# Turning the combine weights and the probabilities by VectorE's 32x32 blocks and transfers instead of TensorE

## The reference, cut to what matters

```python
xn = layernorm(x)
# attention: width 128, window of 32 tokens to either side
h = relu(xn @ nm_w1 + nm_b1);  m = h @ nm_w2 + nm_b2
q, k, v = m @ q_w + q_b, m @ k_w + k_b, m @ v_w + v_b
scores = where(valid, q . k_band / sqrt(128), -inf)
att = softmax(scores) . v_band
# mixture: 16 experts, the best 8 of each token, and a shared one
s = sigmoid(xn @ gate_w.T)
inds = top_k(s + expert_bias, 8)
combine = one_hot(inds) * s / sum(selected s) * 2.826
y = sum_e combine[e] * ((silu(xn @ w_gate[e].T) * (xn @ w_up[e].T)) @ w_down[e].T)
y += (silu(xn @ shared_gate.T) * (xn @ shared_up.T)) @ shared_down.T
out = x + att + y
```

## Time and profile before

| | us |
|---|---|
| median of 3 runs | 737.78 (737.62 to 737.8) |
| the profiled execution's own time | 737.78 |
| its span in the profile | 735.9 |
| PE busy | 717.7 |
| DVE busy | 584.3 |
| ACT busy | 446.5 |
| POOL busy | 356.3 |

### The profile page before, as it was taken

The page is one execution under the profiler, slowest core; times in us unless marked ns, Lnnn a source line. Parts: engine busy times, 40 slices in busy tenths (PEclk is TensorE's granted clock), DMA queues, the critical chain, the costliest instruction groups (busy, mean ns, idle before and its releaser), DMA issues.

```text
span 735.9 us, 10715 instructions
## 1 busy us (share of the span) xinstructions
PE 717.7 (98%) x3448; PEld 581.9 (79%) x3448; DVE 584.3 (79%) x1638; ACT 446.5 (61%) x890; POOL 356.3 (48%) x292
## 2 busy tenths in 40 slices
PE   5889999999999999999999999999999999999998
PEld 5668888788887888888788887888888788887886
DVE  5797878878788787878878788887888878787775
ACT  3666665666557566655666657565655756657473
POOL 3644454444545444464444545445464444545353
PEclk9999999999999999999999999999999999999999
DMA  6604215051330615114051330615125061420500
GB/s 250 260 0 191 84 61 205 9 230 44 148 127 2 232 41 230 45 73 191 12 231 44 158 117 3 240 32 224 51 79 194 1 231 43 159 102 9 236 1 14
DMA packets 23847, 84.72 MB, mean 115 GB/s; under 512 B 2288, under 2 KB 10608, under 8 KB 15600
## 3 DMA queue, kind: packets, MB, share of 16 engines
q1 hardware_dynamic: 23792, 84.04, 30.3%
HBM read 79.32 MB, written 4.72 MB: 114 GB/s over the span
## 4 chain that ended last, share of the span: by engine, by line
PE 91%; DVE 4%; ACT 2%; issue 1%; POOL 1%; DMA 0%; DVEq 0%; ACTq 0%
PE ps_u L381 25%; PE ps_y L391 25%; PE ps_g L371 25%; PE bank L302 3%; PE bank L349 3%; PE bank L330 3%; PE bank L314 2%; PE bank L307 2%; PE bank L339 2%; PE ps_y L358 1%; PE bank L320 1%; DVE ps_u L905 1%; DVE h_lo L911 1%; ACT h_hi L588 1%; ACT prob L569 0%
## 5 line engine op out<-in xcount | busy, mean ns | idle before, releaser
L977 POOL TENSOR_TENSOR silu_c<-silu,comb_b 128x512 f32<-128x512 f32 x256 | 330.2, 1292 | 359.8 <-ACT silu L580 359.4
L588 ACT ACTIVATE h_hi<-ps_u 128x512 fp32r<-128x512 f32 x272 | 162.5, 597 | 270.5 <-DVE ps_u L905 268.0
L911 DVE TENSOR_TENSOR h_lo<-ps_u,h_hi 128x512 fp32r<-128x512 f32 x272 | 186.7, 686 | 68.8 <-ACT h_hi L588 67.6
L905 DVE TENSOR_TENSOR ps_u<-silu_c,ps_u 128x512 f32<-128x512 f32 x256 | 176.5, 690 | 51.5 <-PE ps_u L381 47.4
L580 ACT ACTIVATE silu<-ps_g 128x512 f32<-128x512 f32 x272 | 161.5, 594 | 0.2
L381 PE MATMUL ps_u<-xn_hi,exp_w_hi 128*128 128x512 f32 x272 | 112.6, 414 | 4.2 <-DVE h_lo L911 4.0
L391 PE MATMUL ps_y<-h_hi,exp_w_hi 128*128 128x512 f32 x272 | 113.9, 419 | 0.5 <-DVE h_lo L911 0.4
L371 PE MATMUL ps_g<-xn_hi,exp_w_hi 128*128 128x512 f32 x272 | 109.8, 404 | 0.1
L391 PE MATMUL ps_y<-h_lo,exp_w_hi 128*128 128x512 f32 x272 | 107.9, 397 | 0.0
L371 PE MATMUL ps_g<-xn_hi,exp_w_lo 128*128 128x512 f32 x272 | 107.8, 396 | 0.0
L371 PE MATMUL ps_g<-xn_lo,exp_w_hi 128*128 128x512 f32 x272 | 107.7, 396 | 0.0
(11 more groups left out here) (143 smaller groups left out, 973.2 us busy)
## 6 DMA issues: line engine op xcount, KB each, us to landing
comb_b<-c_dram SPq DMA_DIRECT2D x64, 1024.0 KB, 6.7
xin<-x SPq DMA_DIRECT2D x16, 256.0 KB, 3.3
xres<-x_t SPq DMA_DIRECT2D x16, 256.0 KB, 2.8
out_t<-xres SPq DMA_DIRECT2D x16, 256.0 KB, 2.0
exp_raw<-wexp SPq DMA_DIRECT2D x3, 960.0 KB, 9.1
c_dram<-comb_t SPq DMA_DIRECT2D x16, 32.0 KB, 1.6
exp_raw<-wexp SPq DMA_DIRECT2D x1, 384.0 KB, 5.2
att_raw<-watt SPq DMA_DIRECT2D x1, 330.5 KB, 3.2
```

Source lines behind the costliest of these rows:

```text
L588: A(h_t[hbuf(par, s)][0][:], ps_u[(par + s) % 2][:], ACT.Copy).then_inc(s_h_hi, 1)
L905: V.tensor_tensor(ps_u[i][:], src[:], ps_u[i][:], ALU.mult).then_inc(s_h, 1)
L911: V.tensor_tensor(t[1][:], ps_u[(par + s) % 2][:], t[0][:].bitcast(F32), ALU.subtract)\
L977: G.tensor_tensor(silu_c[i][:], silu[i][:], comb_b[:, s1 - 1, :], ALU.mult).then_inc(s_silu_c, 1)
```

## The change

1. **Combine weights.** `comb_turn` on PE and `comb_out` on ACT go. DVE turns the weights itself, by two transposes in 32x32 blocks at the end of `route_weights` (slot 11 now). SP stores them by four transfers, one for each 32 partitions, to a `c_dram` laid out (2, 32, 2, 128), and `comb_b` is laid out by sequence, then expert.
2. **Probabilities.** `turn_probs` on PE goes. `normalise_probs` writes `prob_n` packed; SP's new `move_blocks` (slot 9, after both sequences are normalised) orders its 32x32 blocks into `prob_k` by 12 transfers; DVE transposes all blocks of both sequences at once (`turn_probs`, slot 12); ACT's `prob_hi` (slot 12) and DVE's `prob_lo` (slot 13) take both sequences in one instruction each, from SBUF.
3. **Key term.** POOL adds the key term to the mask (`mask_terms`, four instructions of 128x160, slots 2 and 3), so that `row_max` gives the negated maximum at once; `full_max` and `neg_max` go.
4. **Slots.** `attend` moves from slots 13 and 14 to 14 and 15, `z_hi` to 16, `z_lo` to slot 0 of the next group, `value_proj` to slot 1; for the last group `z_lo` comes in `finish`, behind `h_prod` and `h_lo` of the last expert. `moments` moves from slot 12 to slot 5, `variance` to 11, the steps of the routing one slot or so later. The key terms are made in two halves, in slots 1 and 2.

```diff
             def store_comb(g, par):
                 sp.wait_ge(S["comb_t"], g + 1)
-                sp.dma_start(c_dram[par * E:(par + 1) * E, :], comb_t[:]).then_inc(s_comb_st[par], 16)
+                for q in range(4):
+                    sp.dma_start(c_dram[par, :, :, q * 32:(q + 1) * 32],
+                                 comb_t[q * 32:(q + 1) * 32, :].rearrange("p (h t) -> p h t", h=2))\
+                        .then_inc(s_comb_st[par], 16)
...
+            def move_blocks(g):
+                def move(q, key, src, dst, each):
+                    a = prob_n[q * HALF:(q + 1) * HALF, :, :].rearrange("p n (t c) -> p (n t) c", t=2)
+                    b = prob_k[key * HALF:(key + 1) * HALF, :, :].rearrange("p n (t c) -> p (n t) c", t=2)
+                    sp.dma_start(b[:, dst // ROOM::each, dst % ROOM:dst % ROOM + HALF],
+                                 a[:, src // ROOM::each, src % ROOM:src % ROOM + HALF]).then_inc(s_blocks, 16)
+                sp.wait_ge(S["pn0"], g + 1)
+                sp.wait_ge(S["pn1"], g + 1)
+                if g > 0:
+                    sp.wait_ge(S["pt"], g)
+                for d in range(3):
+                    for q in range(4):
+                        if 0 <= q + d - 1 < 4:
+                            move(q, q + d - 1, (q + d - 1) * HALF, q * HALF, 1)
+                move(0, 3, WIN, P, 2)
+                move(3, 0, P, WIN, 2)
...
-                if s == 0 and not first(g):
+                if s == 1 and not first(g):
                     value_proj(g - 1)
-                if s == 9:
-                    pe.wait_ge(S["pn1"], g + 1)
-                    turn_probs(1)
-                if s == 13:
+                if s == 14:
                     pe.wait_ge(S["hn_lo"], g + 1)
-                    pe.wait_ge(S["p0_lo"], g + 1)
+                    pe.wait_ge(S["p_lo"], g + 1)
                     attend(0)
...
             def row_max(g, seq):
                 dve.wait_ge(S[f"sc{seq}"], g + 1)
+                dve.wait_ge(S["mask_k"], 2 * g + seq + 1)
...
+                        out=prob[:, n, :], in0=score_bank[seq][:, t * SEQ:t * SEQ + WIN], in1=mask_k[:, n, :],
+                        scale=-1.0, scalar=-TAKEN, op0=ALU.add, op1=ALU.min, accum_out=neg_max[:, n:n + 1])
...
+            def turn_probs(g):
+                dve.wait_ge(s_blocks, MOVES * 16 * (g + 1))
+                V.transpose(prob_t[:], prob_k[:, :, 0:2 * WIN]).then_inc(S["pt"], 1)
...
+                if s == 0:
+                    if not first(g):
+                        z_lo(g - 1)
+                    if more:
+                        normalise(g + 1, 1 - par)
                 if s == 1:
                     hid_n_lo(g)
+                    key_terms(g, 0)
+                if s == 2:
+                    key_terms(g, 1)
+                    if more:
+                        xn_lo(g + 1, 1 - par)
                 if s == 4:
                     row_max(g, 0)
+                if s == 5:
+                    if more:
+                        gate_sum(g + 1)
+                    if more2:
+                        moments(g + 2, par)
                 if s == 6:
                     normalise_probs(g, 0)
+                if s == 7 and more:
+                    route_scores(g + 1)
                 if s == 8:
                     normalise_probs(g, 1)
+                    if more:
+                        route_max(g + 1)
...
+                if s == 11:
                     if more:
+                        route_weights(g + 1, 1 - par)
                     if more2:
                         variance(g + 2)
+                if s == 12:
+                    turn_probs(g)
+                if s == 13:
+                    prob_lo(g)
+                if s == 14 and more:
+                    hid_lo(g + 1)
+                if s == 16 and more:
+                    q_lo(g + 1)
...
+            def mask_terms(g, seq):
+                pool.wait_ge(S["key_term"], 2 * g + seq + 1)
+                for t in range(2):
+                    n = 2 * seq + t
+                    done = G.tensor_scalar(mask_k[:, n, :], mask[:, t, :], key_term[:, n:n + 1], None, ALU.add)
+                done.then_inc(S["mask_k"], 1)
```

More of the change, by code:

```diff
@@ L316, in gate @@
                 done.then_inc(S["gate_mm"], 1)
[L318 to L321, removed]
             def scores(seq):
@@ L332, in scores @@
                 done.then_inc(S[f"sc{seq}"], 1)
[L334 to L337, removed]
-                        c = kb * (SEQ - (P - HALF)) + t * P
-                        done = nc.tensor.transpose(dst[:, c:c + P],
-                                                   prob_n[:, 2 * seq + t, kb * P:(kb + 1) * P], ident[:])
-                done.then_inc(S[f"pt{seq}"], 1)
             def attend(seq):
@@ L473, in att_early @@
                     scores(1)
-                if s == 12 and more:
-                    pe.wait_ge(S["comb"], g + 2)
-                    pe.wait_ge(S["p1_lo"], g + 1)
-                    comb_turn(bank[1])
                 if s == 13 and more:
@@ L537, in gate_exp @@
                 A(flat(gate_e), flat(gate_s), ACT.Exp, scale=-1.0).then_inc(S["gate_e"], 1)
-            def comb_out(g, par):
-                act.wait_ge(S["comb_tp"], g + 1)
-                if not first(g):
-                    act.wait_ge(s_comb_st[1 - par], 8 * (g - 1 + (1 + par)))
-                A(comb_t[:], bank[1][0:E, :], ACT.Copy).then_inc(S["comb_t"], 1)
             def hid_relu(g):
@@ L734, in route_weights @@
                                        op0=ALU.mult, op1=ALU.mult).then_inc(S["comb"], 1)
+                dve.wait_ge(S["comb"], g + 1)
+                if not first(g):
+                    dve.wait_ge(s_comb_st[1 - par], 32 * (g - 1 + (1 + par)))
+                for h in range(2):
+                    done = V.transpose(comb_t[:, h * 32:(h + 1) * 32],
+                                       comb[:].rearrange("p (l h) e -> p h l e", h=2)[:, h, :, :])
+                done.then_inc(S["comb_t"], 1)
             def hid_lo(g):
@@ L752, in hid_n_lo, with key_terms @@
                     .then_inc(S["hn_lo"], 1)
-                if first(g):
+            def key_terms(g, seq):
+                if first(g) and seq == 0:
                     dve.wait_ge(s_row, 1)
                     dve.wait_ge(s_vec2, 1)
-                for a in range(TILES):
+                for a in range(2 * seq, 2 * seq + 2):
                     done = V.tensor_tensor_reduce(
@@ L976, in slot @@
                     pool.wait_ge(s_silu, g1 * STEPS + s1 + 1)
-                    G.tensor_tensor(silu_c[i][:], silu[i][:], comb_b[:, s1 - 1, :], ALU.mult).then_inc(s_silu_c, 1)
+                    G.tensor_tensor(silu_c[i][:].rearrange("p (l x) -> p l x", l=2),
+                                    silu[i][:].rearrange("p (l x) -> p l x", l=2),
+                                    comb_b[:, :, s1 - 1, :], ALU.mult).then_inc(s_silu_c, 1)
                 elif not last(g, 1):
                     inverse_std(g + 2)
+                if s == 2:
+                    mask_terms(g, 0)
+                if s == 3:
+                    mask_terms(g, 1)
             def finish():
```

141 lines of the change are left out of this document (53 added, 88 removed).

## The result

The changed kernel takes 761.24 us (median of 4 runs, 760.9 to 761.79) against 737.76 for the kernel before: ratio 1.0319, interval 1.0301 to 1.0337. I had said 735.5 us, range 726 to 743, and given "slower" 0.28. Its profiled execution took 761.1 us with a span of 759.3, beside 735.9 before, so the trace has to explain 23.4 us.

What follows compares the result with a forecast made beforehand. PE is busy 98%, but waits for ACT or DVE at the removed turns, so little comes off. Terms -5.6 - 0.4 - 1.0 - 0.45 + 2.5 + 2.7 = -2.25 us against 737.78 gave 735.5 us, range 726 to 743.

Steps and rivals of the forecast that it cites:

- Tail: Program end: `value_proj` and all three down products now follow the last `z_lo`; cost 2.7 us (2.0 to 3.0).
- Moments and `xin`: Slot 5: moments need `xin` just as it lands; late loads cost 2.5 us in all (0 to 8).
- All that remains of the change: Gains: 5.6 us in 14 middle groups, 0.4 in the last, 1.0 in group 0, 0.45 in the prologue.
- The first turn: PE's turn ahead of the gate product: removal gains 0, since that product waits for ACT's silu; full worth 0.54 us.
- the second turn: PE's second turn of probabilities: removal gains 0.17 us, not 0.61, as the up product behind waits for `h_lo`.
- The combine weights: PE's turn of them goes, 0.43 us; 0.2 wait at slot 12's up product leaves 0.23 a group.
- the slack: ACT's room behind DVE's moments in slot 5: about 0.4 us; group 4's stall of 1.9 less this loses 1.4.
- My last sign: Middle period in the trace after: 43.7 us right, 42.5 PE's time off in full, 44.1 or more moments or blocks late.
- the new block turns: Rival: DVE's turns cost more than priced, by port contention with POOL or doubled time; 749 us, chance 0.04.
- the cover: Block transfers: PE's up product of slot 13 has about 1 us more, so they are hidden with 1.6 to spare.
- a chance of 0.08: Rival: slower by the blocks; at an issue of 0.8 us each, 766 us; it decides from 0.64; chance 0.08.
- group 0 and the prologue: Group 0, bound by DVE, gains 1.0 us (0 to 2); prologue gains 0.45 as `q_proj` needn't wait for ACT's copy.

Runs made afterwards that it cites:

- The four repairs: The edits of experiment 4, experiment 5, experiment 6 and experiment 8, each run alone on the changed kernel: 750.39, 757.21, 757.78 and 752.71 us.
- experiment 4: Changed kernel with DVE normalising the next group's x ahead of `z_lo` in slot 0, not behind it: 750.39 us, ratio 1.0171.
- experiment 8: Changed kernel with DVE's transpose of the moved blocks behind `h_lo` in slot 12, not ahead of it: 752.71 us, ratio 1.0206.
- experiment 5: Changed kernel with the last group's `z_lo` back in slot 16, ahead of the last `h_prod`: 757.21 us, ratio 1.0258.
- experiment 6: Changed kernel with `moments` and `variance` moved from slots 5 and 11 to slot 15: 757.78 us, ratio 1.0263.
- experiment 10: Changed kernel with the edits of experiment 4, experiment 5, experiment 6 and experiment 8 together: 733.27 us, ratio 0.9941.
- experiment 1: Kernel before, with three of the four matmuls of the first turn (sequence 0, end of slot 7) left out: 737.77 us, ratio 1.0001.
- experiment 7: Changed kernel with 6 of the 12 block transfers left out: 750.13 us, ratio 1.0166.

## Why the prediction was wrong

The four repairs alone save 10.9, 8.5, 4.0 and 3.5 us, 26.9 in all, and 28.0 together. Each is known to 1 to 2.6 us, so an overlap of a few us can't be excluded, but a large one can. That lets the result be set against the sum, part by part:

| Part | Priced, us | Measured, us | By |
|---|---|---|---|
| `z_lo` ahead of the normalisation | 0 | +10.9 | experiment 4 |
| Blocks, with the transpose ahead of `h_lo` | 0 | +8.5 | experiment 8 |
| Tail | +2.7 | +4.0 | experiment 5 |
| Moments and `xin` | +2.5 | +3.5 | experiment 6 |
| All that remains of the change | -7.45 | -4.5 | experiment 10 |
| Sum | -2.25 | +22.4, and +23.5 by the medians | |

**What was right.** The first turn is worth 0 (experiment 1) and PE waits 0.65 us in its place for ACT; the up product behind the second turn and that of slot 12 start on `h_lo`'s end. The combine weights bring 0.16 a group for 0.23. So the step that most of the argument was spent on, that PE's 98% would not come off, held. The step on the moments held in kind and nearly in size: 6 waits and 7.3 us of idle DVE, of which one wait (1.6 us) lies ahead of the first store, where the kernel before has one of 1.4; three of the others make three long periods, 2.7 us, and putting the moments elsewhere gave 3.5. (In its working, 216.79 less 214.9 is 1.9 and not 2.0, and 1.9 less the slack is 1.5 and not 1.4; neither matters.)

**Where it failed first.** "The moved `z_lo`, `attend` and `value_proj` are the same work in slots where PE has 0.5 us or more to spare." I asked of the moved DVE instruction only what it does to PE's room, and not what it pushes back on its own engine. Behind `z_lo` stand the four `xn` instructions, which used to end before POOL's `silu_c` began and now reach into it by one. The fourth lasts 1354 ns for 340, ending with POOL's instruction. The same happened to `weight` (658 ns for 215), but PE's up product behind it waits for nothing in the clean group. My last sign read a middle period of 44.1 us or more as moments or blocks that come late; in the clean groups, at 44.6, it was this (43.75 in experiment 4). The trace of before had a sign of it that I read past: `full_max`, two columns wide, had a mean of 426 ns. It takes 0.16 us at 303.67, with POOL idle, and four times that where `silu_c` runs, ending with it (308.56):

```profile
307.27 1.29 POOL L977 TENSOR_TENSOR silu_c<-silu,comb_b 128x512 f32<-128x512 f32 x1 [1.56 <-ACT silu L580]
...
307.94 0.63 DVE L828 TENSOR_TENSOR full_max<-score_max,key_term 128x2 f32<-128x2 f32 x1
```

The Trainium skill ("Advanced Engine Details and Errata", GPSIMD Details) states it: GpSimd shares a read and a write interface with VectorE and conflicts with VectorE's instructions in a two-port mode or with two SBUF inputs. The trace agrees for `weight` and `full_max` (two SBUF inputs: 658 and up to 1123 ns), and for `xn` (SBUF to SBUF, 1354 ns) if it runs in such a mode, which no row shows. In these rows it is VectorE that waits, until POOL's instruction ends. What the experiments show is the price of the order (experiment 4); that POOL is the cause is read from the ends that coincide, as no run took POOL's instruction away. I had that rule among the rivals only as something that could befall the new block turns (0.04), which it didn't.

**Where it failed next.** "The last is issued 11 x 0.48 = 5.3 us after the first." The 0.47 was of spreads from DRAM; the moves take 0.64, and the last comes 1.8 us later. DVE wanted them 7.97 us after the first issue (325.83 to 333.80), and I had said 7.95. So the lateness at 0.64 follows from my own numbers (7.04 + 1.6 to 2.0, less 7.95, is 0.7 to 1.1; the row shows 0.96). What failed beside the 0.47 is the cover: "PE's up product of slot 13, which has about 1 us more". It hasn't: its weight load waits 0.35 us for `h_lo` in a clean group, and in the six groups whose blocks come 1.6 us late or more PE itself waits 0.6 to 1.8 us. The fixed cost of about 2.0 us that the prediction takes from the Trainium skill ("DMA: Bandwidth & Descriptors", Anatomy of one DMA) is given there for transfers that GpSimd issues; the blocks, which SP issues, landed 1.8 to 3.3 us after their issue, 1.9 in the median, so the landing was not what failed. And the same 0.64 stood in the earlier trace rows for one `xin`; between the two ends I took the low one for the sum and left the high one a chance of 0.08. A step that decides at 0.64, with a measured 0.64 among its rows, is not hidden with 1.6 us to spare.

**Sizes.** The order in the tail cost the 2.7 us that I had priced; what the sum lacked was the fallen clock, 1.4 in this trace. (The 4.0 of the table is what experiment 5 gives back by the medians; its trace shows 3.0.) `mask_terms` costs 0.70 us each, within my bounds of 0.40 and 1.29 but 1.4 us for a pair where I took 0.8, and no wait for it stands in the view of waits; it was not tried alone. The transpose of 640 columns takes 0.845 (0.8), that of `comb` 0.19 each (0.15). The first store comes 2.0 us later where I had group 0 and the prologue gain 1.45; with the repairs it still comes 0.8 later. Why group 0 doesn't gain was not taken apart; what is known is that it is not the combine part, which brings 0.55 there, and not the clock, which is 0.50 from about 49.6 to 53 in this trace but stays at 1.00 there in that of experiment 7, where the first store comes at 82.64.

**The rest of the change.** At -4.5 us (of which the combine weights alone bring 3.0) it is less than the -7.45. Its clean period is better than I said, 43.33 against 44.07, 0.74 us where I had 0.40; but the five periods with late blocks leave 6.9 us of the 10.4 that 14 clean ones would give (I had 5.6), and 0.8 is lost ahead of the first store, where I had a gain of 1.45, and 1.3 in the last group.

## What to carry to other kernels

Before you move a VectorE instruction, list what stands behind it on VectorE and whether GpSimd is busy at the new time. Here an SBUF to SBUF instruction that started 0.6 us later lasted 1.0 us longer. Put a wait for a transfer behind the instruction that feeds the busiest engine, not ahead of it: the same wait then cost 8.5 us less here. And where a threshold computed from rows equals a value that a row shows, treat it as crossed. A time that rests on a single trace should be checked for stretches with a fallen clock first.

## What the runs showed of the hardware

- An `xn` instruction that takes 340 ns lasted 1354 when GpSimd's tensor_tensor started beside it, and ended within 0.1 us of that instruction's end. Instructions of 512 columns with one input in PSUM (`h_prod`, `h_lo`, `z_lo`: 0.68 to 0.70) ran beside it at their usual time.
- An issue on SP's queue took 0.33 us (`c_dram`, before), 0.35 (`out_t`), 0.43 (`xin`), 0.47 (spreads), 0.63 (`c_dram`, in four transfers) and 0.58 to 0.68 for SBUF to SBUF in five shapes.
- In the changed kernel's trace the granted clock was 0.50 from 1.3 us behind PE's restart after a wait of 3.3 us near the end. With the same wait it fell in six of eight traces, from ahead of the restart to 1.3 us behind it, and stayed at 1.00 in two. After a wait of 1.2 us at the same place (experiments 5 and 10) it stayed at 1.00. Earlier in the program it fell twice: during a wait of 2.69 us, at about 49.6, and 1.3 us behind the end of one of 1.78 us, at about 155.5.
